# First attention with its values in four blocks a batch, empty rows stored one batch sooner, and weight products moved behind the first experts

## The chip, the cores and the metric

The kernel runs on one core of a Trainium2 chip. The metric is the device time of one execution in microseconds; the median over several runs counts.

## What is computed

Two layers, each an attention over a context and a layer of experts, on x (16 batches of 112 rows, width 256) and a context of 375 rows a batch:

```python
x = x + L0_xattn(layernorm(x), ctx)          # 16 heads of 16; softmax over own rows and over the context, gated
x = x + L0_ffn(layernorm(x))                 # 8 experts, 256 -> 512 -> 256, the one with the largest router logit
x = x + L1_xattn(ctx, ctx, layernorm(x))     # one head of 256
x = x + L1_ffn(layernorm(x))                 # 16 experts, 256 -> 1024 -> 256, 112 places each

# L0_xattn
dots, dots_aux = q @ k.T * scale, q @ ka.T * scale
out = (softmax(dots) @ v) * (1 - gate) + (softmax(dots_aux) @ va) * gate
return out @ Wo + bo
# L0_ffn
expert_idx = argmax(x @ Wr + br)
y = (relu(x @ W1[e] + b1[e])) @ W2[e] + b2[e]     # for the chosen e
# L1_xattn
qp, kp, vp = q @ Wq.T + bq, k @ Wk.T, v @ Wv.T + bv
```

## The kernel before

Four phases follow one another, with a barrier between them: attention0, ffn0, attention1, ffn1. Each engine has its own program in order; semaphores join them.

attention0 is a software pipeline over 16 batches, written out as steps b = 0 to 20 (unrolled_steps, L113). In step b the projections of batch b are made, the score maxima of batch b-2, the softmax and output of batch b-3, and the router of batch b-4. The TensorE program is `step` at L991:

- First half. `logits(b-3, k)` for 16 groups k of four heads' products (L917) into two alternating PSUM banks (4 and 5), so logits k waits for exponential k-2; `max_scores(b-2, k)` for 8 pairs of heads (L900) into two pairs of banks, so pair k waits for the reductions of pair k-2; `values(b-3, k)` for 16 groups (L932), whose products write 32 rows each at one of four positions. The order is eight times: two logits, one pair of scores, two values of the pair before. The last values stand behind the router's transposes.
- Second half. Transposes of context and x (L981, L1033), of the maxima (L1044), of the values (L874), projections (L1062 to L1069, L987, L1095), router scores (L1324) and counts (L1218, L1219), and the output product (L1113).

ScalarE takes the exponentials (L564) into four buffers `probs`, and copies PSUM results. The vector engine (DVE) reduces the maxima (L776, L777), with the router's statistics (L1286) and normalisation (L1303) set between the reductions, splits them (L789 to L795), normalises the values (L706 to L711) and places rows (L1224 to L1234). GpSimd scatters the rows of a batch by expert into the table sorted0 in DRAM (L1244).

The tiles of an expert are 128 rows, so rows behind an expert's last must be empty. `pad` (L308) stores 240 empty rows for each of 8 experts from the count that is reached after batch 14 (`total`, L936, then `nexts_i`, L834), ScalarE issues three stores and SyncE five; the scatter of batch 15 waits for them. `lay_out` (L714) then makes the table of tiles. In steps 18 and 19 PE also forms products of weights for the second attention (`setup_first`, `setup_rest`, L951, L962), and ScalarE copies them (`setup_copies`, L539). `keep_busy` (L153) issues filler products; one is two records in the trace.

SyncE loads what is needed later in `load_later` (L407): the down weights w2 in two halves, the four weight matrices, small rows, b1, b2.

ffn0 goes over 21 tiles of 128 rows: PE transposes (L1478), multiplies up (L1493) and down (L1506); its program ends with 24 fillers.

## Time and profile before

| what | value |
|---|---|
| median of 3 runs | 772.79 us (769.84 to 773.85) |
| the profiled execution's own time | 771.14 us |
| its span, first to last instruction | 769.3 us |
| PE busy | 720.3 us (94%) |
| DVE, ACT, POOL busy | 419.7, 325.5, 218.0 us |
| mean granted clock of PE | 0.971 |
| attention0 / ffn0 / attention1 / ffn1 begin at | 0 / 432.7 / 528.6 / 644.0 us |
| one step of attention0 in its steady part | 23.4 us |

PE is TensorE, DVE VectorE, ACT ScalarE, POOL GpSimd, SP SyncE; SPq and ACTq are DMA issues by those engines. A timeline row gives start and length in us, engine, line, operation and tiles (out<-in), how many instructions are merged in the row, and in brackets the idle time before it and what ended it. An fp32 product is two records. Lengths of merged rows include the latency of the last product, so distances between starts tell the pace.

### The profile page before, as it was taken

The numbers are of one execution on the slowest core, as the hardware profiler recorded it, in microseconds if no ns is written. First come the engines' busy times: TensorE is split into PE (matmuls) and PEld (weight loads), VectorE is DVE, ScalarE is ACT, GpSimd is POOL, SyncE is SP. The second block draws the span as 40 slices with busy tenths as digits, with TensorE's granted clock in tenths as the row PEclk, the third lists the DMA queues.
The fourth block names the chain that finished last, engine by engine and source line by source line (L and its number), as shares of the span: only waits on it lengthen the run. The fifth ranks groups of instructions, "written<-read, shape, count | busy, mean of one in ns | idle before, by whom it ended". The sixth has DMA issues, their size and how long they took to land. (4 is left out here: it accounts for less than half of the span.)

```text
span 769.3 us, 19472 instructions
## 1 busy us (share of the span) xinstructions
PE 720.3 (94%) x6739; PEld 569.3 (74%) x6740; DVE 419.7 (55%) x1269; ACT 325.5 (42%) x884; POOL 218.0 (28%) x359
## 2 busy tenths in 40 slices
PE   5789999999999999999997898998999989999995
PEld 4457667777667776667665698997788878999994
DVE  4556877778877778776763322222588861111111
ACT  1335665555665556655553143331455540110110
POOL 3212333313333213243110023333356531111111
PEclk8979999999999999999999799999999998999998
DMA  6737554345653446642535459853566633999950
GB/s 173 197 98 195 139 144 107 91 126 166 173 150 103 126 139 174 170 124 74 177 117 156 123 184 259 212 171 104 168 202 217 198 105 111 309 327 342 332 160 17
DMA packets 99527, 128.12 MB, mean 167 GB/s; under 512 B 23394, under 2 KB 84683, under 8 KB 99312
## 3 DMA queue, kind: packets, MB, share of 16 engines
q1 hardware_dynamic: 90193, 115.07, 51.2%
q0 software_dynamic: 3824, 8.46, 3.6%
q10 hardware_dynamic: 5423, 3.48, 1.9%
q8 instruction: 50, 0.82, 0.5%
q14 instruction: 37, 0.30, 0.1%
HBM read 74.68 MB, written 23.88 MB: 128 GB/s over the span
## 5 line engine op out<-in xcount | busy, mean ns | idle before, releaser
L564 ACT ACTIVATE probs<-psum 128x448 f32<-128x448 f32 (+2 forms) x256 | 125.2, 541 | 57.9 <-PE psum L917 57.4
L776 DVE TENSOR_REDUCE neg_max<-psum 112x2 f32<-112x750 f32 x128 | 118.7, 928 | 6.5 <-PE psum L900 4.7
L900 PE MATMUL psum<-stacks 96*128 96x487 bf16 (+1 forms) x256 | 75.5, 377 | 4.6 <-DVE neg_max L777 2.6
L917 PE MATMUL psum<-stacks 102*128 102x112 bf16 (+1 forms) x1024 | 76.9, 214 | 1.6 <-ACT probs L564 0.4
L932 PEld LDWEIGHTS psum<-probs,rings 128*32 128x32 f32 (+2 forms) x2048 | 44.9, 109 | 45.2 <-issue 36.8
L917 PEld LDWEIGHTS psum<-stacks 102*128 102x128 bf16 (+1 forms) x1024 | 54.4, 98 | 30.4 <-ACT probs L564 23.8
L932 PE MATMUL psum<-probs,rings 128*32 128x112 f32 (+2 forms) x2048 | 75.8, 265 | 0.0
L1954 DVE SCALAR_TENSOR_TENSOR e_y<-psum,e_x_in 112x256 f32<-112x256 f32 x16 | 7.7, 484 | 98.0 <-PE psum L2002 98.0
L1988 PEld LDWEIGHTS psum<-e_xt,rings 128*128 128x128 f32 x512 | 59.5, 192 | 2.2 <-ACT e_xt L1934 1.3
L1988 PE MATMUL psum<-e_xt,rings 128*128 128x112 f32 x512 | 59.7, 275 | 0.9 <-ACT e_xt L1934 0.9
L2002 PE MATMUL psum<-rings,e_hid 128*112 128x256 f32 x256 | 57.9, 379 | 1.3 <-DVE e_hid L1961 1.3
L987 PE MATMUL psum<-rings 128*128 128x375 f32 x128 | 48.3, 500 | 5.6 <-ACT xt L575 5.6
L2002 PEld LDWEIGHTS psum<-rings,e_hid 128*112 128x112 f32 x256 | 44.0, 177 | 10.4 <-issue 1.7
L777 DVE TENSOR_REDUCE neg_max<-psum 112x2 f32<-112x224 f32 x128 | 48.4, 378 | 0.0
L1934 ACT COPY e_xt<-psum 128x224 f32<-128x224 f32 x16 | 5.5, 345 | 99.9 <-PE psum L1973 99.9
L1438 ACT ACTIVATE t_hid<-psum,b 128x128 f32<-128x128 f32 x84 | 26.2, 363 | 50.9 <-PE psum L1493 50.9
L1493 PEld LDWEIGHTS psum<-t_xt,t_w 128*128 128x128 f32 x336 | 41.9, 197 | 5.7 <-issue 3.7
L1493 PE MATMUL psum<-t_xt,t_w 128*128 128x128 f32 x336 | 42.8, 283 | 3.4 <-issue 2.7
L1919 POOL DMA_INDIRECT out<-e_y,e_index x16 | 15.2, 951 | 98.7 <-issue 52.8
L444 POOL TENSOR_TENSOR ln_rstd<-ln_mv,eps 112x1 f32<-112x1 f32 x16 | 3.0, 190 | 138.4 <-DVE ln_mv L647 138.4
L1411 POOL DMA_INDIRECT made<-t_y,t_index x21 | 24.2, 1151 | 59.0 <-issue 45.0
L1506 PE MATMUL psum<-stacks,t_hid 128*128 x168 | 40.5, 386 | 0.0
(228 smaller groups left out, 1392.3 us busy)
## 6 DMA issues: line engine op xcount, KB each, us to landing
rings<-in_L_ffn_w SPq DMA_DIRECT2D x32, 1024.0 KB, 7.7
stacks<-rings SPq DMA_DIRECT2D x96, 243.5 KB
ct_dram<-rings SPq DMA_DIRECT2D x16, 375.0 KB, 4.9
a_ct<-ct_dram SPq DMA_DIRECT2D x16, 375.0 KB, 4.4
a_ctx<-in_ctx SPq DMA_DIRECT2D x16, 375.0 KB
stacks<-q_parts SPq DMA_DIRECT2D x93, 56.0 KB
rings<-in_ctx SPq DMA_DIRECT2D x16, 256.0 KB
w<-in_L_ffn_W SPq DMA_DIRECT2D x8, 512.0 KB, 6.2
```

The costliest lines, as they stand in the source:

```text
L564: nc.scalar.activation(probs[k % 4][0:keys, :, :], src, ACT.Exp, scale=DH ** -0.5).then_inc(s["exp_done"], 1)
L776: nc.vector.tensor_reduce(neg_max[:, 0, h:h + 2], psum[0:T, pair:pair + 2, 0:S], AX, ALU.max, negate=True)
L777: nc.vector.tensor_reduce(neg_max[:, 1, h:h + 2], psum[0:T, pair:pair + 2, S:KV], AX, ALU.max, negate=True).then_inc(s["max_done"], 1)
L900: last = nc.tensor.matmul(bank[2 - 2 * (k % 2) + j][0:rows, 0:KV], q_flat[n.third][0:QK, h * T:h * T + rows], k_stack[n.third][0:QK, h, :] ...
L917: last = nc.tensor.matmul(bank[4 + k % 2][0:wide, j * T:(j + 1) * T], k_flat[n.third][:, first:first + wide], q_stack[n.third][:, h, :], s ...
L932: last = nc.tensor.matmul(bank[6 + g // 2][32 * j:32 * j + 32, col:col + T], v[n.parity][0:keys, chunk, h, :], probs[k % 4][0:keys, j, :], ...
L987: last = nc.tensor.matmul(bank[(0, 3)[h]][:, 0:S], w_p[:, a_, 2, h, :], ct[b.parity][:, a_, :], start=(a_ == 0), stop=(a_ == 1))
L1438: nc.scalar.activation(hid[j.parity][:, f, :], up_bank(j, f)[:, f % 2 * P:(f % 2 + 1) * P], ACT.Relu, bias=bias).then_inc(s["hid"], 1)
L1493: last = nc.tensor.matmul(up_bank(j, f)[:, f % 2 * P:(f % 2 + 1) * P], w1_now[j.parity][:, k, f * P:(f + 1) * P], xt2[j.parity][:, k, :], ...
L1506: last = nc.tensor.matmul(bank[6 + n.parity][:, 0:D], hid[n.parity][:, f, :], w2[:, bass.ds(e, 1), f, :].rearrange("p o d -> p (o d)"), st ...
L1988: last = nc.tensor.matmul(bank[2 * e.parity + f // 4][:, f % 4 * C1:(f % 4 + 1) * C1], g.ring1[e.quarter][:, k, f * P:(f + 1) * P], xt[e.p ...
L2002: last = nc.tensor.matmul(bank[6 + n.parity][0:C1, 0:D], hid[n.parity][:, f, :], g.ring2[n.quarter][:, f, :], start=(f == 0), stop=(f == K ...
```

## The change

Six parts:

1. PE's order in the first half (`slots`). Logits 0 and 1 of a batch are issued in the step before, ahead of the output product (`first_logits`); values come in blocks of 3, 4, 3 and 6 groups, `probs` has eight buffers.
2. The router's statistics and normalisation move behind the maxima on DVE, its transposes between two value projections on PE, its counts into the middle of the L1095 products, its copy on ScalarE behind the first copy of v.
3. The total for the empty rows is taken after batch 13 in step 17 and not after batch 14 in step 18; a store covers 352 rows (88 x 4) and SyncE issues all eight, ahead of the second half of w2. The scatter of batch 14 waits for them too.
4. Small rows (bq, bv, bo, Wg, b1) are loaded in step 4.
5. The four weight matrices are loaded in ffn0's steps 8 to 14, and the weight products stand behind its last tile, with 8 fillers for 24.
6. Fillers at the end of attention0: 8 in step 18, 24 (was 4) in step 19.

```diff
+LATE = B - 3
+PROBS = 8
-        PAD = P + T
+        PAD = P + 2 * T
-            empty = g_.empty[0:PAD // 2, :].rearrange("p (o n) -> p o n", o=1).broadcast_to((PAD // 2, 2, ROW0))
+            empty = g_.empty[0:PAD // 4, :].rearrange("p (o n) -> p o n", o=1).broadcast_to((PAD // 4, 4, ROW0))
...
+                if b.c == B + 2:
+                    pad(sp, range(0, 5))
+                if b.c == B + 3:
+                    sp.wait_ge(s["logits_mm"], 16 * B)
+                    pad(sp, range(5, E0))
+                    sp.wait_ge(s_mr[(B - 1) % 2], 16 * (1 + (B - 1) // 2))
+                    load_down(E0 // 2, E0)
...
                 if b.c == B + 3:
                     pool.wait_ge(s["padded"], 16 * E0)
-                if (b - 4).real():
+                    r.scatter(pool, b - 5, r.rows, g_.sorted0, E0 * REGION)
+                if (b - 4).real() and b.c != B + 2:
                     r.scatter(pool, b - 4, r.rows, g_.sorted0, E0 * REGION)
...
-                        act.wait_ge(s["pv_done"], n.count(16, max(k - 3, 0)))
+                        act.wait_ge(s["pv_done"], n.count(16, max(k + 1 - PROBS, 0)))
...
+            def first_logits(n):
+                if n.c == 0:
+                    pe.wait_ge(s["c_ready"], 1)
+                    pe.wait_ge(s["sides_ready"], 48)
+                pe.wait_ge(s_mr[n.parity], n.turn(16, 16))
+                logits(n, 0)
+                logits(n, 1)
+
+            def slots(b):
+                n, ahead = b - 3, b - 2
...
+                if n.c == B - 2:
+                    first_logits(n)
+                if n.c == 0:
+                    pe.wait_ge(s["inv_gate_ready"], 9)
+                for half in range(2):
+                    l, m, v_ = 2 + 7 * half, 4 * half, 7 * half
+                    keys(l, l + 1)
+                    maxima(m, m + 1)
+                    keys(l + 1, l + 2)
+                    maxima(m + 1, m + 2)
+                    keys(l + 2, l + 3)
+                    sums(v_, v_ + 3)
+                    keys(l + 3, l + 5)
+                    maxima(m + 2, m + 4)
+                    keys(l + 5, l + 7)
+                    sums(v_ + 3, v_ + 7)
+                sums(14, 16)
+
             def step(b):
-                for pair in range(8):
-                    if (b - 3).real():
-                        logits(b - 3, 2 * pair)
-                        logits(b - 3, 2 * pair + 1)
-                    if (b - 2).real():
-                        max_scores(b - 2, pair)
-                    if (b - 3).real():
-                        if pair >= 1:
-                            values(b - 3, 2 * pair - 2)
-                            values(b - 3, 2 * pair - 1)
...
+                slots(b)
...
+                if b.real() and (b - 2).real():
+                    first_logits(b - 2)
...
+                        total(b - 4)
+                        g_.keep_busy(bank[4], 24)
...
                     tile_steps(pe, step)
-                    g.keep_busy(bank[0], 24)
+                    setup()
+                    g.keep_busy(bank[0], 8)
```

In the steady part PE's order before, from the output product of one step (L1113) on: logits are L917, scores for the maxima L900, values L932 ("128x112 x8" is two groups of logits, "32x112 x8" two of values).

```order
L1113 MATMUL psum<-wo,mixed 112x256 x2
L917 MATMUL psum<-stacks 128x112 x8
L900 MATMUL psum<-stacks 128x487 x2
L917 MATMUL psum<-stacks 128x112 x8
L900 MATMUL psum<-stacks 128x487 x2
L932 MATMUL psum<-probs,rings 32x112 x8
L917 MATMUL psum<-stacks 128x112 x8
L900 MATMUL psum<-stacks 128x487 x2
L932 MATMUL psum<-probs,rings 32x112 x8
```

The same place now, where the lines are L911 for logits, L892 for scores, L926 for values and L1101 for the output product.

```order
L911 MATMUL psum<-stacks 128x112 x8
L1101 MATMUL psum<-wo,mixed 112x256 x2
L911 MATMUL psum<-stacks 128x112 x4
L892 MATMUL psum<-stacks 128x487 x2
L911 MATMUL psum<-stacks 128x112 x4
L892 MATMUL psum<-stacks 128x487 x2
L911 MATMUL psum<-stacks 128x112 x4
L926 MATMUL psum<-probs,rings 32x112 x12
L911 MATMUL psum<-stacks 128x112 x8
L892 MATMUL psum<-stacks 128x487 x4
L911 MATMUL psum<-stacks 128x112 x8
L926 MATMUL psum<-probs,rings 32x112 x12
```

Two groups of logits moved ahead of the output product, and three or four groups of values stand together where two stood.

SyncE's queue at the end of attention0 before: the down weights (L405), the weight matrices and small rows, then its part of the stores of empty rows (L315), each behind a register load, and b1 and b2.

```order
L405 DMA stacks<-in_L_ffn_W 128x4x256 x8
L420 DMA stacks<-in_L_xattn_Wq 128x2x256
L420 DMA stacks<-in_L_xattn_Wv 128x2x256
L423 DMA stacks<-in_L_xattn_bq 128x1 x2
L313 TENSOR_LOAD nexts_i
L315 DMA sorted<-empty 120x2x257
L427 DMA stacks<-in_L_ffn_b 32x128
L428 DMA stacks<-in_L_ffn_b 128x2048
```

The same queue now.

```order
L406 DMA stacks<-in_L_ffn_W 128x4x256 x4
L314 TENSOR_LOAD nexts_i
L316 DMA sorted<-empty 88x4x257
L406 DMA stacks<-in_L_ffn_W 128x4x256 x4
L427 DMA stacks<-in_L_ffn_b 128x2048
```

All eight stores are in this queue (L314 and L316 stand there eight times), between the two halves of the down weights; the weight matrices are gone from it.

## Rows read from the trace of the kernel before

**Rows 1.** Timeline of PE, first half of one steady step: start us, length us, engine, line, operation

```profile
195.23 0.66 PE L917 MATMUL psum<-stacks 102*128 102x112 bf16 x8
...
197.38 0.59 PE L932 MATMUL psum<-probs,rings 112*32 112x112 f32 x16
197.90 0.57 PE L917 MATMUL psum<-stacks 102*128 102x112 bf16 x8
198.31 0.58 PE L900 MATMUL psum<-stacks 96*128 96x487 bf16 x2
...
206.01 0.78 PE L932 MATMUL psum<-probs,rings 112*32 112x112 f32 x24
206.73 0.54 PE L981 MATMUL psum<-ident,rings 128*128 128x128 f32 x3
207.11 0.36 PE L1310 MATMUL psum<-ident,r_rows 112*128 112x112 f32 x2
...
207.72 0.41 PE L1033 MATMUL psum<-ident,xn 112*128 112x112 f32 x2
...
208.30 0.25 PE L1044 MATMUL psum<-ident,max_parts 112*96 112x112 bf16 x1
```

**Rows 2.** Timeline of DVE in the same stretch

```profile
196.64 0.92 DVE L776 TENSOR_REDUCE neg_max<-psum 112x2 f32<-112x750 f32 x1
...
200.71 0.93 DVE L776 TENSOR_REDUCE neg_max<-psum 112x2 f32<-112x750 f32 x1
...
201.85 0.93 DVE L776 TENSOR_REDUCE neg_max<-psum 112x2 f32<-112x750 f32 x1
...
206.98 0.38 DVE L777 TENSOR_REDUCE neg_max<-psum 112x2 f32<-112x224 f32 x1
```

**Rows 3.** Timeline of ACT in the same stretch

```profile
198.31 0.98 ACT L564 ACTIVATE probs<-psum 112x448 f32<-112x448 f32 x2 [0.70 <-PE psum L917]
```

**Rows 4.** Timeline of PE at the end of attention0

```profile
397.27 0.17 PE L1218 MATMUL psum<-r_onehot,r_before 112*112 112x8 bf16 x1
...
412.51 0.17 PE L1218 MATMUL psum<-r_onehot,r_before 112*112 112x8 bf16 x1
...
413.08 1.99 PE L947 MATMUL psum<-stacks 128*128 128x256 f32 x8
...
420.67 0.91 PE L1324 MATMUL psum<-r_w,r_xt 128*112 128x8 f32 x4 [3.58 <-ACT r_xt L1317]
421.43 2.05 PE L156 MATMUL psum<-ident 128*128 128x128 f32 x8
423.28 0.21 PE L1218 MATMUL psum<-r_onehot,r_before 112*112 112x8 bf16 x1
...
431.07 1.05 PE L156 MATMUL psum<-ident 128*128 128x128 f32 x8
...
435.79 0.44 PE L1478 MATMUL psum<-ident,t_in 128*128 128x128 f32 x2 [1.46 <-DMA t_in<-sorted]
```

**Rows 5.** Timeline of the other engines at the same place

```profile
414.83 8.29 SPq L315 DMA_DIRECT2D sorted<-empty  x5
...
420.27 0.34 ACT L1317 COPY r_xt<-psum 128x224 f32<-128x224 f32 x1 [8.77 <-issue]
...
427.09 0.17 DVE L748 CAST offset_i<-rings 1x21 int32<-1x21 f32 x1
...
427.56 0.99 POOL L1244 DMA_INDIRECT sorted<-r_rows,r_place_i  x1 [11.39 <-DMA sorted<-empty]
```

**Rows 6.** Groups by line, 0 to 420 us: busy us, mean ns | idle before, releaser

```profile
L706 DVE RECIPROCAL inv_sum<-psum 112x16 f32<-112x16 f32 x32 | 8.1, 253 | 21.3 <-PE psum L874 21.3
```

**Rows 7.** Windows, 417 to 419 us: busy us, granted clock, DMA share, GB/s

```profile
417.00:419.00 2.00, 0.08 (x1) 0.00 (x0) 0.00 (x0) 0.00 (x0) 0.00 (x0) 1.00 0.96 282
```

**Rows 8.** Timeline of PE between ffn0 and attention1

```profile
521.54 5.52 PE L156 MATMUL psum<-ident 128*128 128x128 f32 x48
...
528.63 2.47 PE L156 MATMUL psum<-ident 128*128 128x128 f32 x20 [1.56 <-PEq L147]
```

More of the change, by code:

```diff
@@ L281, in attention0 @@
         mt = sb("mt", [QK, T], BF16)
-        probs = [sb(f"probs{k}", [P, 4, T]) for k in range(4)]
+        probs = [sb(f"probs{k}", [P, 4, T]) for k in range(PROBS - 2)] + [early([P, 4, T]) for k in range(2)]
         pv = [sb(f"pv{u}", [P, 2, 2, T]) for u in range(2)]
@@ L938, in total @@
                 pe.wait_ge(r.s["placing"], n.count(3, 1))
-                if n.c == B - 1:
-                    pe.wait_ge(s["nexts_ready"], 1)
-                at = (n.c - (B - 2)) * E0
-                nc.tensor.matmul(bank[7][0:1, at:at + E0], r.ones[:, 0:1], g_.acc[1 - n.parity][:, :], start=True, stop=True).then_inc(s["totals"], 1)
-            def product(to, left, right):
-                for m in range(2):
-                    for k in range(2):
-                        last = nc.tensor.matmul(to[:, m * D:(m + 1) * D], left[:, k, m * P:(m + 1) * P], right[:, k, :],
-                                                start=(k == 0), stop=(k == 1))
-                return last
@@ L951, in setup_first @@
-            def setup_first():
-                weights = g_.weights
-                pe.wait_ge(g_.s_qk, 32)
-                product(bank[2], weights["Wq"], weights["Wk"]).then_inc(s["setup_mm"], 1)
-                pe.wait_ge(g_.s_vo, 32)
-                for k in range(2):
-                    for m in range(2):
-                        last = nc.tensor.transpose(bank[0][:, k * D + m * P:k * D + (m + 1) * P], weights["Wo"][:, m, k * P:(k + 1) * P], ident[:, :])
-                last.then_inc(s["setup_mm"], 1)
@@ L979, in turn_context @@
+                nc.tensor.matmul(to[0:1, 0:E0], r.ones[:, 0:1], g_.acc[1 - n.parity][:, :], start=True, stop=True).then_inc(s["totals"], 1)
             def turn_context(b, h):
@@ new lines, in slots, with keys, maxima, sums @@
+            def slots(b):
+                n, ahead = b - 3, b - 2
+                def keys(first, end):
+                    if n.real():
+                        for k in range(first, end):
+                            logits(n, k)
+                def maxima(first, end):
+                    if ahead.real():
+                        for k in range(first, end):
+                            max_scores(ahead, k)
+                def sums(first, end):
+                    if n.real():
+                        for k in range(first, end):
+                            values(n, k)
+                if n.c == B - 2:
[15 more added lines that the diff above has]
+                sums(14, 16)
@@ L1018, in step @@
                     turn_context(b, 1)
-                if (b - 4).real():
-                    if (b - 3).real():
-                        pe.wait_ge(s["exp_done"], (b - 3).count(16, 15))
+                if (b - 4).real() and not (b - 2).real():
                     r.turn(pe, b - 4, ident)
-                if (b - 3).real():
-                    values(b - 3, 15)
                 if b.real():
@@ L1217, in count @@
             pe.wait_ge(s["placing"], (n - 1).count(PLACING, 2))
-        nc.tensor.matmul(counts, r.before[:, :], r.onehot[:, :], start=True, stop=False)
-        nc.tensor.matmul(counts, r.ones[:, :], acc[n.parity][:, :], start=False, stop=True).then_inc(s["counted"], 1)
+        nc.tensor.matmul(counts(n), r.before[:, :], r.onehot[:, :], start=True, stop=False)
+        nc.tensor.matmul(counts(n), r.ones[:, :], acc[n.parity][:, :], start=False, stop=True).then_inc(s["counted"], 1)
     def place_rows(dve, n, limit=None):
@@ L1224, in place_rows @@
         nc.vector.tensor_tensor(acc[1 - n.parity][:, :], acc[n.parity][:, :], r.onehot[:, :], ALU.add).then_inc(s["placing"], 1)
-        nc.vector.tensor_tensor(r.mine[:, :], counts, r.onehot[:, :], ALU.mult).then_inc(s["placing"], 1)
+        nc.vector.tensor_tensor(r.mine[:, :], counts(n), r.onehot[:, :], ALU.mult).then_inc(s["placing"], 1)
         dve.wait_ge(s["placing"], n.count(PLACING, 2))
@@ L1257, in batch_routing, with router0 @@
     return r
-def router0(nc, g, phase, turn_bank, count_bank):
+def router0(nc, g, phase, turn_bank, counts):
     def sb(name, shape, dt=F32):
@@ L1266, in router0 @@
     scores = turn_bank[0:T, 2 * T:2 * T + E0]
-    r = batch_routing(nc, g, phase, E0, REGION, "r0", lambda n: scores, s["scored"], count_bank[0:T, 0:E0], g.acc)
+    r = batch_routing(nc, g, phase, E0, REGION, "r0", lambda n: scores, s["scored"], counts, g.acc)
     r.w = sb("w", [P, 2, E0])
```

203 lines of the change are left out of this document (112 added, 91 removed).

## The prediction

> **What bounds the kernel now.** I read the page first: TensorE (PE) is busy in almost every slice of the first attention, so the timeline of that engine comes next, over one step of the loop over batches (period 23.4 us). [rows 1] show its first half, where PE alternates between logits (L917), scores for the maxima (L900) and values (L932). The pattern repeats every 1.44 us without a wait (0.41 + 0.51 + 0.52), and three numbers come out of it. Logits: 8 products from 197.90 to 198.31, so 0.20 us for a group of four. Scores: one pair from 198.31; two products of 487 columns stream in 2 x 487 / 2.4 GHz = 0.41 us (the granted clock is 1.00 here), but the values behind them start only 0.51 us later, so entering the values costs 0.10. Values: two groups take 0.52 us (197.38 to 197.90), three take 0.72 (206.01 to 206.73), so 0.20 each and 0.13 for leaving. **One visit to the values costs 0.23 us besides its work**, and a batch has eight: seven in the pairs and the single last group behind the router's transposes.
>
> [rows 2] are the vector engine beside it: a pair of reductions every 1.14 us when it isn't kept waiting, first started 1.41 us after the first logits, last ended at 207.36, and the transposed maxima follow 0.94 later (208.30). ScalarE needs 0.98 us for two exponentials, and begins 0.41 after PE began their logits [rows 3]. So PE leads with 1.44 a pair, the vector engine is only 0.30 behind.
>
> The second place is the end of this attention. [rows 4] (PE) and [rows 5] (the others) show the last batch: its counts at 412.5, eight stores of empty rows from 414.8, issued by SyncE and ScalarE; ScalarE's copy for the router therefore runs at 420.27, although PE had turned its input by 417.09 (its gap of 3.58 ends at 420.67); PE comes back slow, works through weight products and ends at 432.12. The last scatter waits for the empty rows until 427.56.
>
> **The change, part by part.**
>
> Values in four blocks: four visits fewer, 4 x 0.23 = 0.9 us of PE a batch. Two logit groups are issued before the output product of the step before, so the loss at the start (2.15 us from the first logits to the first values against 2 x 0.92 in the steady part, 0.3) goes too. I walked the new order through with the durations above, 0.2 us from a product to its reader, two logit banks and two pairs of score banks. Time 0 is the end of the output product. PE issues logits 2, scores 0, logits 3, scores 1, logits 4 by 1.4; values 0 to 2 from 1.5; logits 5 and 6 from 2.25; scores 2 at 2.65, scores 3 at 3.25 (they wait for the reductions of pair 1); values 3 to 6 from 4.2; scores 4 and 5 at 5.3 and 5.9; values 7 to 9 from 6.6; scores 6 and 7 at 7.7 and 8.3; values 10 to 15 from 9.2 to 10.5. The vector engine starts at 0.8 (its router work at the head of the phase, and the two inserts between pairs 2 and 3 and pairs 6 and 7, have moved), waits 0.6 in all behind the blocks and ends at 10.7. PE then has 0.38 and 0.58 of transposes (206.73 to 207.11, 207.72 to 208.30) and would be at the turned maxima at 11.5; the vector engine allows it at 10.7 + 0.94 = 11.6. Before it was 208.30 - 195.23 = 13.07. **Gain 1.45**, less what only moved: 0.40 for the two logit groups and 0.28 for the router's transposes (207.11 to 207.39): **0.77 a batch**. The same walk with the old order gives 11.5 to the context transposes, as the trace has it.
> Thirteen steps (batches 0 to 12) give 10.0. Step 16 has no transposes of context and gains 1.2; step 17 begins with its logits again and gains 0.5; in step 18 ScalarE and the two banks pace the logits, and both orders take 9.6 to 9.8 in the walk: 0.2 lost. Together **11.5 us**, between nothing (rival A) and 18 (rival C).
>
> At the switch itself a rule bears on this. The Trainium skill (TensorEngine Tiling (Array Packing), Key Properties) says that changing the tiling mode drains the array; its latency formula on the page TensorE: Matmul & The Clock Gate leaves some 0.17 us per drain, so 0.33 a visit, an estimate by which a batch would gain 0.4 more and the sum be 749. The measured 0.23 holds both ends of a visit, and I take that.
>
> Router work on the vector engine (statistics and normalisation of 0.4 each, with small ones some 1.1 together) moves to both sides of the attention's normalisation, ahead of which that engine idles 21.3 us in 32 times, 1.3 a batch [rows 6], waiting for PE. So it costs nothing there; without that cover up to 1.1 a batch. The small loads of step 4 (seven issues of 0.4 to 0.5 on SyncE) stand before copies that are read two steps later: zero; if that cover failed, 3 us once.
>
> Empty rows a batch sooner: nexts are ready with the counts of step 17 (397.27 in the old time), so the stores start 2.3 us later, as they did before (412.51 to 414.83), 15.2 us sooner. They are larger, 352 rows for 240, 2.9 MB for 1.9. SyncE alone issues them, 8.29 / 5 = 1.66 us each, 13.3 in all; the 282 GB/s of [rows 7] would need 10.3. They land some 4.5 after the last issue, 4.9 us after the last batch's counts (call that C). Slower engines or a queue behind them could make it C + 9, and then the next phase would start one or two later.
> The Trainium skill (DMA: Bandwidth & Descriptors, the section on why a DMA increments by 16) lets a transfer use the largest number of engines up to 16 that divides its outer dimension: 15 for the old 120, 11 for the new 88. Twice the rows per engine would put the landing at about C + 8, an estimate that takes 1 us off this term.
>
> ScalarE is now free for the router: statistics come 0.7 sooner (ahead of the placing), so the rows are turned by C + 3.9 (before C + 4.6), the scores start at C + 4.4, the one-hot 1.6 later, counts at C + 6.2, the layout of the tiles done 3.98 later (423.28 to 427.26) at C + 10.2. The last scatter is issued at C + 7.2 and lands before C + 12. PE has no weight products left, but 24 filler products after the total, 48 records, 5.5 us by [rows 8]: it ends last, at C + 12.3. Before it was 432.12 = C + 19.6. **Gain 7.3**; behind it the second half of the down weights and b2 (3 MB, queued behind the stores) must land. At the same rate that takes until C + 15 or 16; the first tile used to arrive 3.7 after PE's end (435.79), now C + 16. It just fits: I take **7.2**.
>
> Behind the experts: four transposes, two products of 2.0 us (413.08), the two thin ones about 1.7, and 8 fillers (1.8), together 7.6 in place of 5.5, so PE ends at 529.2 instead of 527.06 [rows 8]. The next phase started 1.57 after PE, and in the other change of phase 0.6 (432.12 to ffn0's start at 432.7): between +0.6 and +2.1, I take **+1.5**.
>
> Sum: -11.5 - 7.2 + 1.5 = -17.2. The profiled execution took 771.1 by its own time (span 769.3), so 753.9; the median of the three runs stands 1.7 above it: **755 us**.
>
> **Rivals.**
>
> A, the attention gains nothing: the vector engine's idle time behind blocks grows to what the drains gave. For it: only 0.30 a pair lie between it and PE; against it: 1.14 x 8 + 0.8 = 9.9 leaves room. Then 772.8 - 5.7 = 767.
>
> B, the end gains little: PE idles in pieces after the last batch, as it did before its granted clock went to 0.50 (the filler records at 421.43 took 0.26 each, those of [rows 8] 0.115). At double the 0.115 the 48 fillers would take 5.5 longer, C + 17.8, gain 1.8: 761. The same if the down weights behind the stores come 5 late. For it: the fall after 3.6 us of idleness; against it: eight fillers now stand in the gap.
>
> C, more: the waits of my walk (0.4 of PE a batch) don't come about: 755 - 6 = 749.
>
> D, slower: each values block starves the vector engine for its whole length (three of 0.7 to 0.9), and each double pair of scores then waits a reduction more, since scores 2 and 3 want banks just released: 3.3 us idle a batch, not 0.6, which is 15 x 2.7 = 40 lost against 17 won, 796. It decides from 1.15 us of extra idleness a batch. Against it: PE issues two pairs close together before each block, which is over a microsecond of supply.
>
> E, the change doesn't do what it says: the early stores are held up by SyncE's queue and the end stays, 762.
>
> **How the numbers follow.** Forecast 0.50, A 0.13, B 0.17, C 0.09, D 0.05, E 0.06. The range of 747 to 765 leaves out D and most of A. A measurement of this kernel tells a change from none at about 0.5%, 3.9 us. Faster by more than that are all but D and a part of A: 0.90; within it 0.05, slower 0.05.
>
> **What would show it.** Step period 22.6 for 23.4; four blocks of values a batch with exits of 0.13; the turned maxima 11.6 after the output product, with PE and the vector engine arriving together; the empty rows landed before the last batch is counted; no ScalarE gap before its router copy, and a clock of 1.00 there; PE's gap between the phases earlier by 7. Wrong: waits of PE on the reductions longer than 0.5 a batch, fillers at half clock, or a first tile that waits for down weights.

## The result, and the profile after

| | before | after |
|---|---|---|
| median of the runs made together | 771.53 us (4 runs) | 764.29 us (762.42 to 764.95, 4 runs) |
| profiled execution, span | 769.3 us | 762.5 us |
| mean granted clock | 0.971 | 0.965 |
| counts of step 18 (L1218, now L1210) | 412.51 us | 412.33 us |
| ffn0 / attention1 / ffn1 begin at | 432.75 / 528.63 / 644.02 us | 426.25 / 521.81 / 637.16 us |

The ratio is 0.9896 with an interval of 0.9862 to 0.993: the change makes the kernel faster, by 5 to 11 us, but not by the 17 that were forecast. The two spans are 6.8 apart. The most telling line of the table is that of the counts. They are the router's counts in step 18, which the prediction calls C and "the last batch's"; they belong to batch 14, and those of batch 15 follow in step 19, 5.5 us later in the changed kernel. "The counts" are those of step 18 from here on. The first attention reaches them 0.2 us sooner than before, where 11.5 were forecast.

Where did that go? First the steady step, in the timeline of TensorE after the change (start, length, engine, line, operation, tiles, count, and in brackets the idle time before and what ended it). It answers to [rows 1]:

```profile
192.18 0.36 PE L911 MATMUL psum<-stacks 102*128 102x112 bf16 x4
...
193.70 0.78 PE L926 MATMUL psum<-probs,rings 112*32 112x112 f32 x24
194.42 0.57 PE L911 MATMUL psum<-stacks 102*128 102x112 bf16 x8
...
196.35 0.79 PE L926 MATMUL psum<-probs,rings 119*32 119x112 f32 x24
...
198.79 0.40 PE L926 MATMUL psum<-rings 119*32 119x112 f32 x8
...
201.44 0.98 PE L926 MATMUL psum<-probs,rings 128*32 128x112 f32 x32
...
203.86 0.25 PE L1022 MATMUL psum<-ident,max_parts 112*96 112x112 bf16 x1
```

The output product ends at about 192.15. The four blocks of values (L926) start 1.55, 4.20, 6.64 and 9.29 behind it, where the walk had 1.5, 4.2, 6.6 and 9.2, and the turned maxima (L1022) 11.7 behind it, where it had 11.6. They stand 22.63 apart from step to step, before 23.39. The forecast of the steady part holds to 0.02 us a batch.

The loss is in steps 17 and 18, in which the batches run out. The same view for TensorE there:

```profile
383.27 0.25 PE L1022 MATMUL psum<-ident,max_parts 112*96 112x112 bf16 x1 [1.05 <-DVE max_parts L777]
...
384.23 0.61 PE L158 MATMUL psum<-ident 128*128 128x128 f32 x4
387.00 0.41 PE L1302 MATMUL psum<-ident,r_rows 112*128 112x112 f32 x2 [2.15 <-DVE r_rows L1295]
387.84 0.91 PE L1316 MATMUL psum<-r_w,r_xt 128*112 128x8 f32 x4 [0.43 <-ACT r_xt L1309]
...
392.44 0.21 PE L1210 MATMUL psum<-r_onehot,r_before 112*112 112x8 bf16 x1
...
394.78 1.35 PE L926 MATMUL psum<-probs,rings 112*32 112x112 f32 x24
...
412.33 0.17 PE L1210 MATMUL psum<-r_onehot,r_before 112*112 112x8 bf16 x1
...
418.46 7.16 PE L158 MATMUL psum<-ident 128*128 128x128 f32 x48
426.25 1.58 PE L158 MATMUL psum<-ident 128*128 128x128 f32 x12 [0.63 <-PEq L149]
429.28 0.44 PE L1494 MATMUL psum<-ident,t_in 128*128 128x128 f32 x2 [1.46 <-DMA t_in<-sorted]
```

In step 17 TensorE stands idle for 2.15 us ahead of the router's transposes (L1302), and from there everything is slow: a block of three groups of values takes 1.35 (394.78), in the steady step 0.78. Why it waits stands in the vector engine's timeline:

```profile
384.89 0.77 DVE L698 TENSOR_TENSOR mixed_rows<-normed 112x128 f32<-112x128 f32 x1
...
386.53 0.41 DVE L1295 TENSOR_SCALAR r_rows<-xs,r_mv,r_deviation 112x256 f32<-112x256 f32 x1
```

The router's normalisation (L1295) now stands behind that of the attention. In the other steps its reader on TensorE comes behind two value projections; in step 17 there is no batch left to project, and the reader waits. How it stands with the clock is seen in a table of stretches (busy time of TensorE, its weight loads, DVE, ACT and POOL, then the granted clock, the DMA engines' busy share, GB/s):

```profile
373.00:380.00 7.00, 6.95 (x131) 4.55 (x129) 6.61 (x13) 4.95 (x11) 0.00 (x0) 1.00 0.13 40
380.00:387.00 7.00, 3.79 (x72) 3.07 (x72) 6.34 (x18) 2.49 (x6) 1.79 (x7) 1.00 0.02 5
387.00:393.00 6.00, 5.31 (x26) 4.42 (x26) 1.22 (x9) 1.83 (x5) 0.00 (x0) 0.55 0.00 1
393.00:400.00 7.00, 6.47 (x88) 4.87 (x89) 1.84 (x9) 3.48 (x7) 1.76 (x3) 0.50 0.45 121
400.00:407.00 7.00, 6.47 (x100) 5.18 (x98) 0.00 (x0) 3.90 (x8) 0.00 (x0) 0.50 0.58 168
407.00:413.00 6.00, 5.73 (x46) 4.83 (x39) 3.19 (x13) 1.38 (x4) 0.00 (x0) 0.91 0.74 190
...
418.00:426.00 8.00, 7.36 (x51) 7.07 (x50) 3.31 (x18) 0.00 (x0) 0.94 (x1) 0.79 0.56 214
```

TensorE is busy for 3.79 of the 7 us up to 387, and the granted clock, 1.00 until then, is at the lower of its two levels (1.2 GHz) for the next 20 us. From the turned maxima of step 17 to the counts it took 29.06 us (383.27 to 412.33). In the trace of before the same stretch is 392.75 to 412.51, 19.76. **The difference of 9.3 us is nearly all that the thirteen steady steps had won.**

```profile
392.75 0.25 PE L1044 MATMUL psum<-ident,max_parts 112*96 112x112 bf16 x1 [0.83 <-DVE max_parts L795]
```

The ledger of the two spans, from such marks (after less before):

| stretch | us |
|---|---|
| to the turned maxima of step 2 (44.70, 45.39) | +0.7 |
| thirteen steps, to those of step 15 | -9.7 |
| steps 15 to 17 | -0.5 |
| from there to the counts | +9.3 |
| counts to the start of ffn0 (20.24, 13.92) | -6.3 |
| ffn0 to its last down product | -2.2 |
| behind the experts, to attention1 | +1.9 |
| attention1 and ffn1 | 0.0 |

The first line is the spread of single executions: in the kernels below the first maxima stand between 42.98 and 46.54. Half of the -2.2 belongs to the clock: ffn0's first tile takes 2.0 us for its up products now, 3.05 before, as TensorE no longer comes out of a slow stretch, and the third tile's transposes stand 1.1 sooner behind the start of ffn0 (8.96 for 10.02). The other 1.2 lie behind that tile, in pauses whose sum differs from one execution to the next: from the third tile's transposes to the last one's it is 71.59 before and 70.41 after, and between 69.4 and 72.7 in the kernels below. They can't be put down to the change. The first tile's up products, after and before:

```profile
430.23 2.02 PE L1509 MATMUL psum<-t_xt,t_w 128*128 128x128 f32 x16 [0.51 <-issue]
```
```profile
436.75 3.05 PE L1493 MATMUL psum<-t_xt,t_w 128*128 128x128 f32 x16 [0.51 <-issue]
```

### The profile page after: what moved, and what is told of

It is laid out like the page before. It is cut to its first block and busy times, and to the rows that moved or that the text cites. A ratio compares the mean times of both kernels' runs of the same rounds, so it can differ in the third digit from the quotient of the medians.

```text
span 762.5 us, 19483 instructions
## 1 busy us (share of the span) xinstructions
PE 712.6 (93%) x6753; PEld 581.2 (76%) x6754; DVE 424.1 (56%) x1269; ACT 333.1 (44%) x884; POOL 216.4 (28%) x359
## 5 line engine op out<-in xcount | busy, mean ns | idle before, releaser
L758 DVE TENSOR_REDUCE neg_max<-psum 112x2 f32<-112x750 f32 x128 | 119.6, 934 | 10.4 <-PE psum L892 8.4
L552 ACT ACTIVATE probs<-psum 112x448 f32<-112x448 f32 (+1 forms) x192 | 100.4, 542 | 35.4 <-PE psum L911 29.9
L911 PEld LDWEIGHTS psum<-stacks 102*128 102x128 bf16 (+1 forms) x1024 | 64.6, 101 | 39.4 <-ACT probs L552 13.0
L911 PE MATMUL psum<-stacks 102*128 102x112 bf16 (+1 forms) x1024 | 82.5, 218 | 2.3 <-ACT probs L552 2.3
L892 PE MATMUL psum<-stacks 96*128 96x487 bf16 (+1 forms) x256 | 76.9, 383 | 3.7 <-DVE neg_max L759 1.4
L926 PE MATMUL psum<-probs,rings 128*32 128x112 f32 (+2 forms) x1536 | 52.2, 270 | 0.0
L2047 PEld LDWEIGHTS psum<-rings,e_hid 128*112 128x112 f32 x256 | 44.0, 177 | 10.4 <-issue 1.7
L158 PE MATMUL psum<-ident 128*128 128x128 f32 x244 | 37.6, 315 | 4.9 <-PEq L149 2.9
L926 PEld LDWEIGHTS psum<-probs,rings 128*32 128x32 f32 (+2 forms) x1536 | 37.7, 113 | 4.6 <-issue 0.3
```

The costliest lines, as they stand in the source:

```text
L158: nc.tensor.matmul(to[:, 0:P], g.ident[:, :], g.ident[:, :], start=True, stop=True)
L552: nc.scalar.activation(probs[k % PROBS][0:keys, :, :], src, ACT.Exp, scale=DH ** -0.5).then_inc(s["exp_done"], 1)
L758: nc.vector.tensor_reduce(neg_max[:, 0, h:h + 2], psum[0:T, pair:pair + 2, 0:S], AX, ALU.max, negate=True)
L892: last = nc.tensor.matmul(bank[2 - 2 * (k % 2) + j][0:rows, 0:KV], q_flat[n.third][0:QK, h * T:h * T + rows], k_stack[n.third][0:QK, h, :] ...
L911: last = nc.tensor.matmul(bank[4 + k % 2][0:wide, j * T:(j + 1) * T], k_flat[n.third][:, first:first + wide], q_stack[n.third][:, h, :], s ...
L926: last = nc.tensor.matmul(bank[6 + g // 2][32 * j:32 * j + 32, col:col + T], v[n.parity][0:keys, chunk, h, :], probs[k % PROBS][0:keys, j, ...
```

## The experiments

Ten kernels were run. The first four undo or move one thing each in the changed kernel, the others go on from the kernel that is named with them. Line numbers differ by a few.

**Router of step 17 in its old place.** Three engines keep the new order of the router in every step but 17:

```diff
-                if (b - 4).real() and (b - 2).real():
+                if (b - 4).real() and (b - 1).real():
                     r.copy_in(act, b - 4)
...
-                elif (b - 2).real():
-                    r.turn(pe, b - 4, ident)
```

(and likewise for the statistics, the normalisation and the transposes).

> The changed kernel, with the router's statistics, normalisation, transposes and copy of step 17 alone (the step that has no value projections) back where they stood before the change; all other steps stay as changed. Theory: in the changed trace PE waits 2.15 us for the normalised rows at 387.0, its granted clock is 0.50 from then to about 407, and so the last two steps of the first attention lose 9.3 us against the kernel before. With the rows normalised between the reductions PE has no such wait, the clock stays at 1.00, steps 17 and 18 take 34.5 to 35.5 us from turned maxima of step 17 to the counts of step 18 minus what the early logits save (29.1 in the changed trace, 19.8 before: expect 19.5 to 20.5), and the time is 755 to 756.5. Rival 1: the clock falls anyway, from the gaps in step 18; then the wait alone is won, and the time is 761 to 762. Rival 2: the slow stretch comes from the new block order in step 18 itself; the time stays at 763 to 765.

Measured: 760.34 us, ratio 0.985 (0.9818 to 0.9882). TensorE's timeline:

```profile
381.01 0.25 PE L1022 MATMUL psum<-ident,max_parts 112*96 112x112 bf16 x1 [0.93 <-DVE max_parts L777]
...
382.42 0.47 PE L1314 MATMUL psum<-r_w,r_xt 128*112 128x8 f32 x4
...
400.55 0.17 PE L1208 MATMUL psum<-r_onehot,r_before 112*112 112x8 bf16 x1
...
406.68 5.62 PE L158 MATMUL psum<-ident 128*128 128x128 f32 x48
417.57 2.90 PE L158 MATMUL psum<-ident 128*128 128x128 f32 x12 [5.26 <-PEq L149]
...
421.87 3.75 PE L1507 MATMUL psum<-t_xt,t_w 128*128 128x128 f32 x16 [0.51 <-issue]
```

The stretch from the maxima of step 17 to the counts is 19.54 us (381.01 to 400.55): **the 9.3 us are gone**, and the clock stays at 1.00 up to there. But the time misses the 755 to 756.5 that were expected. A new wait shows behind the fillers: TensorE is done at 412.3, 11.8 behind the counts, and is let into ffn0 only at 417.57, 17.0 behind them. In the idle time the clock falls, and the first tile's up products take 3.75 us.

**Fillers in the wait.** The wait stays, TensorE is kept busy in it:

```diff
                 elif (b - 2).real():
+                    g_.keep_busy(bank[2], 10)
                     r.turn(pe, b - 4, ident)
+                    g_.keep_busy(bank[2], 2)
```

> The changed kernel with 10 filler products ahead of the router's transposes in step 17 and 2 behind them; order and waits are untouched. It separates the wait from the clock. Theory: of the 9.3 us lost in steps 17 and 18 about 3 are the wait for the normalised rows, which stays, and about 6 are the half clock behind it, which goes: 757.5 to 759.5, granted clock 1.00 from 387 to 407. Rival: the loss is the wait and the order, the clock only goes along: 763 to 765, whatever the clock shows.

Measured: 763.63 us, 0.9888 (0.9856 to 0.9919), so not measurably other than the changed kernel, where 757.5 to 759.5 were expected. The total alone would speak for the rival, but the trace doesn't:

```profile
381.57 0.25 PE L1022 MATMUL psum<-ident,max_parts 112*96 112x112 bf16 x1 [1.05 <-DVE max_parts L777]
...
382.54 2.84 PE L158 MATMUL psum<-ident 128*128 128x128 f32 x24
385.31 0.41 PE L1304 MATMUL psum<-ident,r_rows 112*128 112x112 f32 x2
...
388.72 0.17 PE L1212 MATMUL psum<-r_onehot,r_before 112*112 112x8 bf16 x1
...
421.46 2.90 PE L158 MATMUL psum<-ident 128*128 128x128 f32 x12 [4.49 <-PEq L149]
```

From the maxima of step 17 to the counts (403.73) are 22.16 us at a clock of 1.00. The changed kernel takes 29.06 and the kernel above 19.54, and the 9.5 between them are divided by this: the wait itself is 2.6 (22.16 less 19.54), **the clock that fell behind it 6.9** (29.06 less 22.16). At the end of the attention a part of that gain is lost again: ffn0 begins 17.7 behind the counts, 13.9 in the changed kernel.

**Eight visits to the values again**, with single groups of logits between:

```diff
-                    sums(v_, v_ + 3)
-                    keys(l + 3, l + 5)
+                    sums(v_, v_ + 2)
+                    keys(l + 3, l + 4)
+                    sums(v_ + 2, v_ + 3)
+                    keys(l + 4, l + 5)
```

(the block of four likewise in two).

> The changed kernel with its four visits to the values split into eight by single groups of logits (2, 1, 2, 2, 2, 1, 2, 4 groups); scores, logits, values and everything else stay in their order otherwise. Theory (PE's visits at 0.23 us set the steady step, with the vector engine close behind): my walk gives PE's end of the first half at 11.2 for 10.5 and the turned maxima at 12.15 for 11.6: the step grows from 22.64 to 23.1 to 23.3, time +7 to +10. Rival: the vector engine's reductions set the step and visits are free now: 22.64 to 22.75, time +0 to +1.5.

Measured: 773.46 us, 1.0018 (0.9993 to 1.0044), 9.2 more than the changed kernel, where 7 to 10 were expected. The turned maxima:

```profile
183.50 0.25 PE L1026 MATMUL psum<-ident,max_parts 112*96 112x112 bf16 x1
...
206.66 0.25 PE L1026 MATMUL psum<-ident,max_parts 112*96 112x112 bf16 x1
```

They stand 23.16 apart, 0.53 more than with four visits, as the walk with 0.23 a visit had it (23.1 to 23.3; part of the 0.9 is taken up where TensorE would have waited for the vector engine). So the visits account for 0.53 of the 0.76 that the steady step gained. The rest wasn't taken apart further than in the next kernel.

**Router between the reductions in every step**, all its parts in the old order but the counts.

> The changed kernel with the router's statistics and normalisation between the reductions, its transposes ahead of the turned maxima and its copy ahead of them in every step, as before the change (counts stay moved). Theory: the inserts of 0.66 and 0.40 us on the vector engine now matter, since it ends the first half together with PE; the walk gives 12.05 for 11.6 to the turned maxima, less 0.28 of transposes that leave the second half: a step of 22.8. Steps 17 and 18 lose their wait as in the first experiment: 757 to 758.5. Rival: the vector engine has the room, the step stays at 22.64 or falls to 22.4: 752 to 756.

Measured once: 762.6 us. Its steady step is 22.78, 0.15 longer than with the router moved, so the move is worth 0.15 x 14 = 2 us in the steps in which it has cover, and costs 9.2 by the step in which it has none (9.5 behind the maxima of step 17, less 0.35 that the old place costs ahead of them: 43.66 from step 15's to step 17's in the changed kernel, 44.01 in the first experiment). The steady part came as expected (22.8), the total didn't (757 to 758.5), for the same reason as above: ffn0 began 17.8 behind the counts (402.88 to 420.66).

**What holds the phase.** In all of these the attention's end ran up against something that didn't show in the changed kernel, whose slow step 18 had hidden it. The last work on GpSimd in the kernel with the router of step 17 in its old place, and the stretches around it:

```profile
407.81 0.99 POOL L1234 DMA_INDIRECT sorted<-r_rows,r_place_i  x1 [4.83 <-DVE r_place_i L1224]
409.10 0.94 POOL L1234 DMA_INDIRECT sorted<-r_rows,r_place_i  x1 [0.30 <-issue]
```
```profile
410.00:412.00 2.00, 2.00 (x20) 2.00 (x19) 0.08 (x1) 0.00 (x0) 0.05 (x1) 1.00 1.11 415
412.00:414.00 2.00, 0.31 (x3) 0.12 (x2) 0.00 (x0) 0.00 (x0) 0.00 (x0) 1.00 0.77 314
414.00:416.00 2.00, 0.00 (x0) 0.00 (x0) 0.00 (x0) 0.00 (x0) 0.00 (x0) 0.88 0.10 40
```

GpSimd ends the phase by waiting for its scatters. The last is issued at 409.10, ffn0 begins 8.5 later; before the change it was 5.2 (427.56 in [rows 5] to 432.75) and in the changed kernel 6.6 (419.67 to 426.25), though in both TensorE ended only 0.6 ahead of ffn0 and the scatter may have landed sooner. In between the DMA engines move 314 to 415 GB/s: the second half of the down weights (2 MB) and b2 (1 MB), queued behind the empty rows, are on their way just when the last rows are scattered. The traffic ends at 414.9, 2.7 us before ffn0.

**Down weights and b2 in ffn0.** In the kernel with the router of step 17 in its old place both are loaded from the start of ffn0, behind the first four tiles, and nothing stands behind the empty rows:

```diff
-                    load_down(E0 // 2, E0)
-                    sp.dma_start(g_.b2, ...)
...
                     for c in range(4):
                         load(Item(0, c, TILES))
+                    for e in range(E0 // 2, E0):
+                        sp.dma_start(g.w2[:, e, :, :], ...)
+                    sp.dma_start(g.b2, ...)
```

> The router of step 17 in its old place, as in e1_router17 (760.3), and beside it the second half of the first experts' down weights (4 loads, 2 MB) and their biases (1 MB broadcast) are loaded from the start of the experts' phase, behind its first four tiles, no longer behind the empty rows at the end of the attention. Theory: in e1_router17 the phase changed 17.0 us after the last batch's first counts (400.55 to 417.57) though TensorE was done at 11.8, because the last two scatters (407.81 and 409.10) landed late behind those 3 MB (8.4 us from the last scatter to the new phase, where the kernel before took 5.2 with nothing else on its way, and the changed kernel 6.6). Then the phase changes 13.8 to 15.2 after the counts, 1.8 to 3.2 earlier, and the time is 757 to 758.5. Rival 1: two scatters 1.3 us apart take 8.4 whatever else is moved; then 760.3 stays. Rival 2: the weights now arrive too late for the first down product (it waits for all eight), which stood 11 us after the change of phase; then the gain is spent there and TensorE waits for the loads.

Measured: 767.14 us, 0.9948 (0.9926 to 0.9969), not 757 to 758.5.

```profile
416.01 1.58 PE L158 MATMUL psum<-ident 128*128 128x128 f32 x12 [0.63 <-PEq L149]
...
431.71 3.78 PE L1507 MATMUL psum<-t_xt,t_w 128*128 128x128 f32 x16 [12.19 <-DMA stacks<-in_L_ffn_W]
```

The theory and the second rival both came true, the total missed. ffn0 begins 12.45 behind the counts (403.56), as soon as TensorE is done, which shows that the loads had held the phase. And the first up product waits 12.2 us for the weights, which costs more than it brought.

**Empty rows as 32 x 11.** The same, with stores of 32 partitions and 11 rows instead of 88 and 4:

```diff
-            empty = g_.empty[0:PAD // 4, :] ... broadcast_to((PAD // 4, 4, ROW0))
+            empty = g_.empty[0:32, :] ... broadcast_to((32, PAD // 32, ROW0))
...
-                places = ....rearrange("(o p) n -> p o n", o=4)
+                places = ....rearrange("(o p) n -> p o n", p=32)
```

> As e8_down_late, and the 352 empty rows of an expert are stored as 32 partitions of 11 rows, not as 88 partitions of 4. Theory: while the stores alone are on their way in e1_router17 the DMA engines' busy share is 0.71 to 0.74 (some 11 of 16) at 199 to 217 GB/s, one store leaves SyncE's queue every 1.54 us, and the last lands at about 407.8; the Trainium skill (DMA: Bandwidth & Descriptors, on why a DMA increments its semaphore by 16) gives 11 engines to an outer size of 88 and 16 to one of 32. So the share becomes about 1.0, the eight stores take 11/16 of their 20 us, all have landed about 12 to 13 after the first is issued (3 or more before the last batch's place is known at 6.5 behind the counts), the scatter of batch 14 goes at once and that of batch 15 at 6.7 behind the counts; the phase changes when TensorE's fillers are done, 12.4 to 13.3 behind the counts, 1.5 to 2.5 earlier than in e8_down_late: 754.5 to 757. Rival: the share stays 0.7 (it is not the outer size that sets it), and the time is that of e8_down_late within 0.5.

Measured: 768.11 us, 0.9957 (0.994 to 0.9975), not 754.5 to 757 and not measurably other than the kernel above. A stretch in which only the stores are on their way, first with 88 x 4 (the kernel above):

```profile
394.00:398.00 4.00, 3.06 (x70) 2.23 (x71) 0.00 (x0) 3.25 (x7) 0.00 (x0) 1.00 0.74 205
```

and then with 32 x 11:

```profile
394.00:398.00 4.00, 3.06 (x65) 2.21 (x64) 0.00 (x0) 3.03 (x7) 0.00 (x0) 1.00 1.01 202
```

The share goes from 0.74 to 1.01, and the bytes per second don't move. The stores leave SyncE's queue in 13.1 us instead of 12.4, and from the first of them to the scatter that waits for all it is 17.9 instead of 18.5. The share came as expected, the time that was to follow from it didn't: more busy time of the DMA engines carries the same stream. What sets the rate stays open. The edit changes two things at once, the busy share and the number of partitions that are read (88 or 32), and in the kernel before, two queues with stores of 120 x 2 rows moved 282 GB/s at a share of 0.96 ([rows 7]).

**No fillers at the end of ffn0** (the call behind `setup()` taken out of the kernel above).

> As e9_stores32, without the 8 calls of fillers (16 instructions, 1.95 us in the changed kernel) behind the weight products at the end of the first experts' phase. Theory: they are the last work of the phase on any engine (the next phase begins 1.4 us behind their end), so that the second attention begins 1.4 to 1.95 earlier and the time falls by as much, if the clock stays at 1.00 over the gap. Rival 1: the granted clock falls in the gap and the second attention gives the gain back (0 to 2 us slower than the theory). Rival 2: something else holds the change of phase (the result row's load): no change.

Measured: 766.94 us, 0.9948 (0.9926 to 0.997), within the uncertainty of the kernel above. With the fillers, then without:

```profile
527.94 2.47 PE L158 MATMUL psum<-ident 128*128 128x128 f32 x20 [1.43 <-PEq L149]
```
```profile
523.58 4.10 PE L158 MATMUL psum<-ident 128*128 128x128 f32 x20 [2.06 <-PEq L149]
```

From the first weight transposes to the change of phase it is 7.86 us instead of 9.01, but the next phase's own fillers now take 4.10 instead of 2.47. To attention1's first product behind its transposes it is 12.58 instead of 12.68: rival 1, the gain is given back in clock (granted 0.50 from 525 to 527, 1.00 with the fillers).

**8 fillers for 24 at the end of the attention**, in the kernel with 32 x 11 stores.

> As e9_stores32, with 8 instead of 24 calls of fillers at the end of the attention (32 of 48 instructions, 3.7 us at full clock). Theory: there the last scatter's landing (5.2 us behind its issue at 6.7 to 7.7 behind the counts, so 12 to 13) ends at about the same time as the fillers (11.8), so their removal brings the change of phase forward by 0 to 0.5 us, and the 4 us in which TensorE then stands idle cost clock: the first tiles run at 0.5 (the first tile's up products 3.75 us as in e1_router17 instead of 2.02), 0.5 to 3 us slower than e9_stores32. Rival: the fillers are what holds the phase; then it changes up to 3.7 earlier and the kernel is faster by 1 to 3.

Measured: 764.84 us, 0.9924 (0.9897 to 0.9951). It was expected to be slower, and the median is 3 us lower; the two intervals still touch.

```profile
414.91 2.90 PE L158 MATMUL psum<-ident 128*128 128x128 f32 x12 [3.98 <-PEq L149]
```

ffn0 begins 12.19 behind the counts (402.72 to 414.91) with TensorE idle for 3.98 before it, with all fillers 12.38: so here the landing of the last scatter (issued at 410.09, 4.8 before ffn0 begins) holds the phase at about the same point as the fillers, and they can be left out at no cost to it. Here, too, the traffic of the DMA engines ends 2.7 us before ffn0 (412.2). In the trace the lower time comes from elsewhere: the wait for the weights was 9.75 instead of 11.83, the second tile ran at the full clock, and the pauses behind the third tile were 2.2 shorter. Whether that was the fillers' doing or the spread of single executions wasn't separated.

**b2 alone in ffn0.** Of the 3 MB behind the empty rows only the 1 MB of b2 is moved, in the kernel with the router of step 17 in its old place:

```diff
                     load_down(E0 // 2, E0)
-                    sp.dma_start(g_.b2, ...)
...
                     for c in range(4):
                         load(Item(0, c, TILES))
+                    sp.dma_start(g.b2, ...)
```

> As e1_router17 (router of step 17 in its old place, 760.3), and of the 3 MB that stand behind the empty rows only the 1 MB of the biases (b2, broadcast) is moved, to the start of the experts' phase behind the first four tiles; the down weights stay. Theory, after e8_down_late, where the phase changed at 12.45 behind the last counts with nothing behind the empty rows, and the first tile then waited 12.2 us for weights: the landing of the last scatter is held by what stands behind the empty rows, at some 0.9 us for 0.36 MB, so the phase changes 2.4 to 3.2 earlier than the 17.0 of e1_router17: 13.8 to 14.6 behind the counts. The first tile finds its weights, DVE needs the biases only behind the first down product (some 12 us into the phase). 757 to 758.5. Rival: DVE waits for the biases (they land 8 to 10 us after their issue, between the next tiles' loads): the gain is lost in the first two tiles, 760.

Measured: 758.12 us, 0.9811 (0.9788 to 0.9835), as expected (757 to 758.5). It is the lowest median of this study and, by intervals that don't touch, faster than both the kernel before and the changed one; the 2.2 us to the first experiment (760.34) lie within the intervals.

```profile
418.99 1.89 PE L158 MATMUL psum<-ident 128*128 128x128 f32 x12 [2.55 <-PEq L149]
...
423.10 3.75 PE L1507 MATMUL psum<-t_xt,t_w 128*128 128x128 f32 x16 [0.51 <-issue]
```

ffn0 begins 14.3 behind the counts (404.65), 2.7 sooner than the 17.0 with b2 ahead, as the theory had it, and 6.2 after the last scatter's issue (412.80). DVE doesn't wait for b2: its first wait for a down product is 4.40 us, as in the first experiment.

**Down weights beside the last scatter.** As above, with the down weights issued when the last places are known, and awaited only ahead of the first down product:

```diff
+                    sp.wait_ge(r.placed, B)
                     load_down(E0 // 2, E0)
...
-                    pe.wait_ge(g.s_w2, 16 * E0)
...
+                        if not j.looped() and j.c == 1:
+                            pe.wait_ge(g.s_w2, 16 * E0)
```

> As e12_biases_late, and the last 2 MB of down weights are issued only when the last batch's places are known (6.5 behind the counts), beside the last scatter, and TensorE waits for them just ahead of the first down product, no longer ahead of the first up product. Theory: the last two scatters then share the DMA engines with little that is ahead of them, the phase changes 12.4 to 13.5 behind the counts, and the weights land some 8 us after their issue, 14 to 16 behind the counts and 6 or more before the first down product (some 8 us into the phase): 755.5 to 757.5. Rival: the scatters are overtaken by the 2 MB (written in 112 small rows each, they are served between the large ones) and land as late as in e12_biases_late: 757 to 758.5.

Measured: 760.08 us, 0.9841 (0.982 to 0.9862), above the 755.5 to 757.5 expected, though not clear of the kernel above. ffn0 begins 16.4 behind the counts (402.52 to 418.93), 9.0 after the last scatter was issued at 409.93: worse than the rival had it. The loads' issues began at 409.11, so that all 2 MB were on their way beside the scatter; in the kernel above they were issued from 404.71, and by the GB/s of the stretches behind the last scatter's issue (0.87 MB, the scatters included) about two thirds of them had landed by then, an estimate.

## Why the prediction was wrong

**The steady step was right** in its gain, in its walk and in its cause (0.77 forecast, 0.76 measured; with eight visits again 23.16, which is 0.53 of it). Thirteen steps brought 9.7 for 10.0. Rivals A and D are refuted by that: the vector engine's waits didn't take up the gain.

**The step that failed** is the one that costed the router's moved work: "So it costs nothing there; without that cover up to 1.1 a batch", together with "step 17 begins with its logits again and gains 0.5; in step 18 ... 0.2 lost". The cover was priced for the steady step and not looked for in step 17, where no projection is left behind which the router's transposes could wait. The price was wrong too. The wait costs 2.6 and not 1.1, since all of the attention's normalisation stands ahead, and the clock that fell behind it costs 6.9. For steps 16 to 18 together the forecast had -1.5 (-1.2, -0.5 and +0.2); measured were -0.5 and +9.3. Undoing the one part gives 9.2 us back (29.06 to 19.54, less 0.35 ahead of it), which leaves -0.4 of the -1.5.

The missing 1.1 is a second error, of size. Step 16 gained 0.5 for 1.2 (23.37 to 22.86) and step 17 nothing for 0.5 (20.78 to 20.80). In both TensorE waits for the vector engine's maxima, 0.83 us before and 1.05 now (the rows of 392.75 and 383.27). In these two steps the vector engine ends last, and what TensorE saves ahead of it is spent in that wait.

**The end of the attention**: forecast 7.2, measured 6.3. TensorE does end last, at 13.3 behind the counts instead of 12.3, though the DMA engines' traffic ends at 423.4, 2.9 before ffn0, hardly sooner than where it holds the phase (2.7). The 48 records of fillers took 7.16 us and not 5.5, at a granted clock of 0.79 (rival B's mechanism, at a third of its size). The chain up to them came as written: scores 3.8 behind the counts (4.4 forecast), batch 15's counts 5.5 (6.2), the last scatter 7.3 (7.2). What the text took for just fitting, the 3 MB behind the stores, does fit here, but only since step 18 ran slow and gave the stores 5 us more. With a step 18 at full clock they hold the phase to 17.0; the text had asked of them only that they land before the first tile. So the two terms were not independent. Only where nothing stands behind the empty rows does TensorE end the phase as forecast: it is done 11.8 behind the counts, and ffn0 begins 12.4 to 12.5 behind them.

**The landing of the stores**: forecast 4.9 behind the counts. The scatter that waits for all of them was issued at 3.6 behind them in the changed kernel (415.92), and at 7.3 in the kernel with step 18 at full clock (407.81, beside 400.55), at 5.9 there with nothing behind the stores (409.41, beside 403.56). The first looks better than the forecast by luck: the stores had 5 us more. At full clock the term was 1.0 to 2.4 too small.

**At the switch of tiling** the text chose 0.23 a visit and not 0.33, and 755 instead of 749. The step of 22.63 agrees with 0.23; the experiment with eight visits, in which waits hide a part, fits it and doesn't measure it. The Trainium skill (TensorEngine Tiling (Array Packing), Key Properties) says that each change of mode drains the array. The traces show a cost at both ends of a visit, 0.10 and 0.13, which agrees; the estimate from its pages, 0.33, was too high here.

**At the stores** the Trainium skill (DMA: Bandwidth & Descriptors, the section on why a DMA increments its semaphore by 16) is borne out in the number of engines: shares of 0.74 and 1.01 for outer sizes of 88 and 32, against 11/16 and 16/16 by its rule. The old stores, of 120, had 0.96 against 15/16. That fewer engines take longer isn't borne out by the kernel with 32 x 11: 205 and 202 GB/s. The landing, 5.9 behind the counts without the loads and 7.3 with them, lies between the forecast of 4.9 and the 8 of that estimate.

**Behind the experts**: forecast +1.5, measured +1.9 (6.92 from the last down product's end to attention1 before, 8.84 after). The forecast had not foreseen that ffn0's first tiles would gain 1.1 from the clock.

Against the span of before the sum was -17.2 and came to -6.8: of the missing 10.4 us 10.3 are steps 16 to 18, 0.9 the end of the attention, 0.7 the start of the execution (which is spread), 0.3 the steady steps and 0.4 the end of ffn0; the 2.2 that nobody had forecast in ffn0 go the other way. (The text's 753.9 and the 1.7 of the median make 755.6, which it gives as 755.) None of the rivals was what happened. The time of 764.29 lies inside the range, at its edge, by luck: none of the reasons that the range was made of came true.

## What to carry to other kernels

When work is moved to where something covers it, look for the cover in every step of the pipeline, above all in the last ones, in which batches run out: an order that wins 0.15 us in each of fourteen steps lost 9.2 by one. A wait of TensorE late in a phase should be priced at the wait and at the clock behind it. And a gain ahead of a phase change brings the loads and scatters there closer together: order what the barrier waits for ahead of what only the next phase needs, as with the 1 MB of b2, which was worth 2.7 us at that place in the traces (17.0 to 14.3).

## What was not expected of the hardware

- The granted clock fell from 1.00 to 0.50 behind a stretch in which TensorE was busy for 3.79 of 7 us, idle for 1.05 and 2.15. It then stayed at 0.50 through 20 us, though TensorE was busy for 6.47 of 7 us in two stretches of them. In the kernel with fillers in the wait it didn't fall.
- Stores of rows of 1 KB from one queue moved 202 to 205 GB/s whether 0.74 or 1.01 of the DMA engines' time was busy; from two queues, with 120 partitions, 282 at 0.96.
- The phase that waits for a scatter of 112 rows began 4.8 us after its issue with nothing else on its way, 6.2 after it behind 2 MB of loads of which about two thirds had landed, and 8.5 to 9.0 after it beside 2 to 3 MB.
